# A gated attention and expert block on one core: last steps written out, last roots on VectorE, 77 tiles for 80, first steps reordered

## The reference

```python
# attention, 16 heads of 64, each sequence over its own 64 context rows
q, k, v = layer_norm(layernorm(x)) @ Wq, layer_norm(ctx) @ Wk, layer_norm(ctx) @ Wv
x = x + tanh(g_xattn) * (softmax(q @ k.T / 8) @ v) @ Wo
# one expert of 14 for each token
h = layernorm(x)
e = argmax(h @ router_w); w = softmax(h @ router_w)[e]
x = x + tanh(g_ffn) * w * (gelu(h @ w1[e] + b1[e]) @ w2[e] + b2[e])
```

## Time and profile before

| what | value |
|---|---|
| median of 3 runs | 816.81 us (815.28 to 817.33) |
| the profiled execution | 818.13 us |
| its span, from the first to the last instruction | 816.4 us |
| busy share: PE, PEld | 91%, 84% |
| busy share: DVE, ACT, POOL | 72%, 70%, 60% |
| mean granted TensorE clock | 0.951 of full speed |
| written to and read from memory | 44 MB, 54 GB/s in the mean |

### The profile page before, as it was taken

One profiled execution on the slowest core, in us unless ns is written; L12 is line 12 of the kernel. 1 busy time (PEld: TensorE's weight loads), 2 busy tenths in 40 slices (PEclk: granted clock), 3 DMA queues, 4 the chain that ended last, 5 costly groups with the idle time before them and its releaser, 6 DMA issues. The chain is left out here.

```text
span 816.4 us, 34986 instructions
## 1 busy us (share of the span) xinstructions
PE 746.2 (91%) x12705; PEld 689.3 (84%) x12706; DVE 584.5 (72%) x1580; ACT 571.3 (70%) x1180; POOL 488.4 (60%) x1071
## 2 busy tenths in 40 slices
PE   6779999999999999999999999999999864688884
PEld 6569999999999999999999999999999753588884
DVE  5356678787778787777778787877777853477774
ACT  4557878777778787777787878778877541366663
POOL 2534566666666666666666666666666553277777
PEclk9889999999999999999999999999999965699997
DMA  4840011111101110010010111111000000464540
GB/s 125 235 138 19 20 34 34 31 31 31 31 31 31 31 31 31 31 31 31 31 37 31 37 31 33 36 34 32 25 22 22 23 15 26 127 172 142 143 140 18
DMA packets 50525, 43.90 MB, mean 54 GB/s; under 512 B 14632, under 2 KB 46026, under 8 KB 50474
## 3 DMA queue, kind: packets, MB, share of 16 engines
q1 hardware_dynamic: 43898, 30.53, 13.6%
q0 software_dynamic: 5632, 12.67, 4.4%
q10 hardware_dynamic: 944, 0.01, 0.1%
HBM read 28.55 MB, written 15.68 MB: 54 GB/s over the span
## 5 line engine op out<-in xcount | busy, mean ns | idle before, releaser
L450 POOL TENSOR_TENSOR probs<-probs,row_inv 128x1024 f32<-128x1024 f32 x64 | 122.0, 1907 | 47.2 <-DVE row_inv L1066 46.5
L570 ACT ACTIVATE KT<-psJ 128x512 f32<-128x512 f32 x128 | 76.2, 595 | 56.3 <-PE psJ L742 53.4
L1061 DVE TENSOR_REDUCE row_sum<-probs 128x16 f32<-128x1024 f32 x64 | 77.7, 1215 | 39.0 <-ACT probs L616 39.0
L610 ACT ACTIVATE PTs<-psT 128x512 f32<-128x512 f32 x128 | 75.9, 593 | 37.0 <-PE psT L836 37.0
L1074 DVE TENSOR_TENSOR OT_l<-psO,OT_h 128x1024 fp32r<-128x1024 f32 x64 | 78.1, 1221 | 24.8 <-ACT OT_h L603 24.8
L570 ACT ACTIVATE V<-psJ 128x512 f32<-128x512 f32 x128 | 73.1, 598 | 26.1 <-PE psJ L742 22.8
L616 ACT ACTIVATE probs<-probs 128x1024 f32<-128x1024 f32 x64 | 67.8, 1060 | 24.3 <-DVE probs L1053 24.2
L1046 DVE TENSOR_REDUCE row_max<-psS 128x16 f32<-128x1024 f32 x64 | 75.6, 1181 | 10.1 <-PE psS L799 10.1
L836 PE MATMUL psT<-ident,probs 128*128 128x128 f32 x512 | 79.3, 277 | 3.2 <-POOL probs L450 2.4
L740 PE MATMUL psJ<-CT_h,Wk_h 96*128 96x256 f32 x256 | 78.4, 306 | 2.7 <-ACT QT L570 2.1
L740 PE MATMUL psJ<-XT_h,Wq_h 128*128 128x256 f32 x256 | 77.8, 304 | 3.2 <-ACT QT L570 3.1
(11 more groups left out here) (202 smaller groups left out, 2193.8 us busy)
## 6 DMA issues: line engine op xcount, KB each, us to landing
V<-rows_by_expert SPq DMA_DIRECT2D x40, 129.0 KB
QT<-rows_by_expert SPq DMA_DIRECT2D x40, 129.0 KB, 2.1
x_in<-in_x_dram SPq DMA_DIRECT2D x32, 128.0 KB, 2.1
x_res<-in_x_dram SPq DMA_DIRECT2D x32, 128.0 KB, 2.1
c_in<-in_ctx_dram SPq DMA_DIRECT2D x32, 96.0 KB, 2.3
rows_by_expert<-pad_row SPq DMA_DIRECT2D x1, 1806.0 KB, 11.7
w_sb<-in_L_ffn_w_dram SPq DMA_DIRECT2D x1, 1792.0 KB, 9.6
rows_by_expert<-rows,place_i POOLq DMA_INDIRECT x64, 2.6
```

The source lines that it names most:

```text
L450: pool.tensor_tensor(pr, pr, row_inv[:, p.k % 2, :].unsqueeze(2).to_broadcast([P, 16, SEQ]), ALU.mult).then_inc(s_norm, 1)
L570: act.activation(dst, psJ[n % 2][:, :], ACT.Copy).then_inc(s_jobev, 1)
L610: act.activation(PTs[:, (p.k - 1) % 2, half, :], psT[:, :], ACT.Copy).then_inc(s_ptev, 1)
L1061: dve.tensor_reduce(row_sum[:, :], pr, AX.X, ALU.add).then_inc(s_sum, 1)
```

## The change

It has four parts.

1. **First steps.** In step 0 ScalarE copies jobs 0 and 1 before `norm_in`, and VectorE does `scores_max` and `scores_sub` before `stats_in` and `means_in`. The split of the output weights moves from the end of step 0 to the end of step 2, with raw weights in a buffer of their own, and TensorE's wait for it from the start of step 1 to just before `out_proj` of step 3.
2. **Last steps.** Steps 62 and 63 get an order of their own on TensorE, step 63 on ScalarE too, and steps 64 to 69 are written out piece by piece on all engines (`D64` to `D69`). `router` and `rank` of group 29 and `post_b`, `router` and `rank` of group 30 work in the bank `psJ[1]`, which the jobs no longer need.
3. **Last roots.** The roots of groups 30 and 31 are taken by VectorE (`last_roots`: 12 instructions on two columns) and no longer by GpSimd.
4. **77 tiles.** `TILES` is the most that 8192 tokens in 14 experts can fill, 77, and no longer rounded up to 80: one trip written out, three in the loop, and 13 tiles with the drain written out.

The function `spin` (products on the identity, to keep TensorE at work) is only moved; it is called ahead of the front part, as before, and nowhere behind it.

```diff
-    TILES = -(-(TOK // P + E - 1) // RING) * RING
+    TILES = (TOK + E * (P - 1)) // P
+    TRIPS = TILES // RING
...
-        raw_v, raw_o = Vf[0:C, HALF:HALF + INNER], Vf[:, HALF + INNER:HALF + 2 * INNER]
+        raw_v, raw_o = Vf[0:C, HALF:HALF + INNER], sb("raw_o", [P, M8 * D])[:, :]
...
-            for u in range(LOOP_TO, STEPS_U):
+            for u in range(LOOP_TO, GROUPS // 2):
...
+        D64, D65, D66, D67, D68, D69 = (Plan(GROUPS // 2 + n // 4, n % 4) for n in range(6))
...
-            with eng.Fori(1, TILES // RING) as v:
+            with eng.Fori(1, TRIPS) as v:
...
-            words = entries(engine, expert_tab, TILES // PACK - 1, 1, 2 ** 16 - 1)
-            for i in range(4):
-                ffn(TILES + i, TILES // RING, i, [i - n < 0 for n in range(5)], experts(words, i))
+            words = entries(engine, expert_tab, TRIPS * (RING // PACK) - 1, RING // PACK + 1, 2 ** 16 - 1)
+            for t in range(TRIPS * RING, TILES + 4):
+                ffn(t, t // RING, t % RING, [t - n < TILES for n in range(5)], experts(words, t - TRIPS * RING))
...
@@ GpSimd @@
+            send(D65)
+            send(D67)
+            send(D69)
+            with pool.Fori(0, TRIPS) as v:
                 for i in range(RING):
                     send_out(v * RING + i, i, v)
+            for t in range(TRIPS * RING, TILES):
+                send_out(t, t % RING, TRIPS)
...
@@ ScalarE, norm_x2 @@
+                if p.fixed and p.g >= GROUPS:
+                    bias, scale = shift4[p.g - GROUPS][:, 0:2], rstd4[p.g - GROUPS][:, 0:2]
+                    act.wait_ge(s_rootx, 13 * (p.g - GROUPS + 1))
...
@@ ScalarE, step @@
-                if p.odd:
+                if p.fixed and p.s == PAIRS - 1:
+                    norm_x2(p)
+                    values_high(p)
+                    probs_out(p, 0)
+                    probs_out(p, 1)
+                    norm_T(p)
+                    expo(p)
+                    attn_out(p)
+                elif p.odd:
...
-                    norm_in(p)
+                    if not (p.fixed and p.s == 0):
+                        norm_in(p)
                     values_high(p)
                     job(p, 0)
                     job(p, 1)
+                    if p.fixed and p.s == 0:
+                        norm_in(p)
                     expo(p)
...
-                    if p.fixed and p.s == 0:
+                    if p.fixed and p.s == 2:
                         high(3)
...
@@ ScalarE, behind the front part's steps @@
+            values_high(D64)
+            route_exp(D64)
+            probs_out(D64, 0)
+            probs_out(D64, 1)
+            values_high(D65)
+            norm_x2(D65)
+            attn_out(D65)
+            norm_T(D65, psJ[1])
+            route_exp(D66)
+            norm_x2(D67)
+            norm_T(D67)
+            route_exp(D68)
...
@@ TensorE, step @@
-                    if p.fixed and p.s == 1:
-                        pe.wait_ge(s_wl, 4)
+                if p.fixed and p.s == PAIRS - 1:
+                    scores(p)
+                    value_sums(p)
+                    probs_T(p, 0)
+                    probs_T(p, 1)
+                    post_b(p)
+                    out_proj(p)
+                elif p.fixed and p.s == PAIRS - 2:
+                    scores(p)
+                    value_sums(p)
+                    pe.wait_ge(s_jobev, 12 * GROUPS)
+                    post_a(p)
+                    probs_T(p, 0)
+                    router(p)
+                    probs_T(p, 1)
+                    rank(p)
...
+                    if p.fixed and p.s == 3:
+                        pe.wait_ge(s_wl, 4)
                     out_proj(p)
...
@@ TensorE, behind the front part's steps @@
+            misc[1] = (s_jobev, 12 * GROUPS)
+            value_sums(D64)
+            post_a(D64)
+            router(D64, 1)
+            probs_T(D64, 0)
+            probs_T(D64, 1)
+            rank(D64, 1)
+            value_sums(D65)
+            out_proj(D65)
+            post_b(D65, 1)
+            post_a(D66)
+            router(D66, 1)
+            rank(D66, 1)
             pe.wait_ge(s_bias, 32)
             pe.wait_ge(s_ptev, 2 * PAIRS)
             pe.transpose(psT[:, 0:E * FK], b1_rows[:, :], ident[0:E * FK, 0:E * FK]).then_inc(s_b1T, 1)
+            post_b(D67)
+            router(D68)
+            rank(D68)
+            misc_free()
...
@@ VectorE, step @@
-                    stats_in(p)
-                    means_in(p)
+                    if not (p.fixed and p.s == 0):
+                        stats_in(p)
+                        means_in(p)
                     scores_max(p)
                     scores_sub(p)
+                    if p.fixed and p.s == 0:
+                        stats_in(p)
+                        means_in(p)
...
-                    if p.fixed and p.s == 0:
+                    if p.fixed and p.s == 2:
                         low(3)
...
+            def last_roots(p):
+                i = p.g - GROUPS
+                nw0, nq0, rstd0, shift0, n = nw4[i][:, 0:2], nq4[i][:, 0:2], rstd4[i][:, 0:2], shift4[i][:, 0:2], 13 * i
+                dve.wait_ge(s_agg2, 2 * (p.g - 1))
+                dve.tensor_scalar(nw0, mv[:, 4:6, 1], EPS, None, ALU.add).then_inc(s_rootx, 1)
+                dve.wait_ge(s_rootx, n + 1)
+                dve.tensor_scalar(rstd0.bitcast(I32), nw0.bitcast(I32), -0.5, RSQRT_SEED, ALU.mult, ALU.add).then_inc(s_rootx, 1)
...
@@ VectorE, behind the front part's steps @@
+            values_low(D64)
+            residual(D64)
+            means_x2(D64)
+            route(D64, psJ[1])
+            places(D64, psJ[1])
+            weight(D65)
+            values_low(D65)
+            last_roots(D64)
+            residual(D66)
+            means_x2(D66)
+            last_roots(D66)
+            route(D66, psJ[1])
+            places(D66, psJ[1])
+            weight(D67)
+            route(D68)
+            places(D68)
+            weight(D69)
```

More of the change, by code:

```diff
@@ L363, in load_rows, with load_trip @@
                 sp.dma_start(tile_rows[i], rows_dram[bass.ds(r, P), :]).then_inc(f_load[i], 16)
-            def load_trip(v):
-                for i in range(RING):
+            def load_trip(v, count):
+                for i in range(count):
                     if i % PACK == 0:
@@ L623, in attn_out, with norm_T @@
                 act.activation(aT[:, :], psM[:, 0:GT], ACT.Copy, scale=tanhs[:, 0:1]).then_inc(s_aT, 1)
-            def norm_T(p):
+            def norm_T(p, bank=psM):
                 if p.group(2) is None:
@@ L862, in post_a, with post_b @@
                 misc[0] = (s_x2, p.g - 1)
-            def post_b(p):
+            def post_b(p, b=0):
                 if p.group(2) is None:
                     return
-                misc_free()
+                misc_free(b)
                 pe.wait_ge(s_n2, 2 * (p.g - 1))
                 for t in range(2):
-                    last = pe.transpose(psM[:, P * t:P * t + P], rows[:, p.par(), t, D:2 * D], ident[:, :])
+                    last = pe.transpose(banks[b][:, P * t:P * t + P], rows[:, p.par(), t, D:2 * D], ident[:, :])
@@ L898, in step, with spin @@
+            def spin(n, bank):
+                for _ in range(n):
+                    pe.matmul(bank[:, 0:P], ident[:, :], ident[:, :], start=True, stop=True)
             def step(p):
@@ L935, in step @@
                     job(p, 7)
-            def spin(n):
-                for _ in range(n):
-                    pe.matmul(psO[:, 0:P], ident[:, :], ident[:, :], start=True, stop=True)
             pe.wait_ge(s_cc, 2)
-            spin(13)
+            spin(13, psO)
             prep(Plan(-1, 0))
-            spin(10)
+            spin(10, psO)
             for n in range(10):
@@ L1138, in weight, with places @@
                 dve.tensor_scalar(rows[:, par, :, 2 * D], inv[:, :], tanhs[:, 1:2], None, ALU.mult).then_inc(s_route, 1)
-            def places(p):
+            def places(p, bank=psM):
                 if p.group(3) is None:
```

80 lines of the change are left out of this document (48 added, 32 removed).

## The result

| | median | runs | ratio to before, 95% interval |
|---|---|---|---|
| before | 816.04 us (814.69 to 817.33) | 4 | |
| after | 806.91 us (806.71 to 807.31) | 4 | 0.9889 (0.9870 to 0.9908) |

The change takes 9.1 us off; 806.1 was predicted.

What follows compares the result with a forecast made beforehand. TensorE was taken to set the pace from 56 to 640 us, GpSimd's scatters the end. -6.5 - 0.3 - 3.9 = -10.7 us from the profiled 818.13 gives 807.4, as median 806.1 us; range 804 to 808.5, chance 0.60.

Steps and rivals of the forecast that it cites:

- The start, -6.5 forecast: Steps 0 to 3: earlier job 4, no stand for `Wo_l` and less half clock take 6.5 us off.
- the lower of the two sums, 5.7: Start: 1.7 (job 4) + 3.0 (`Wo_l` stand) + 1.0 (clock), if the first half-clock stretch still ends at 43.3.
- The upper sum, 7.2: Start: up to 1.5 us more than 5.7, if the first half-clock stretch ends earlier.
- the warning that a gain beyond 7 us would run into the load of group 4: Step 2: its next load, `x_in` and `c_in`, is behind the pad rows and would limit a start gain beyond 7 us.
- part of the start only: Rival: lower clock case (5.7), and a load or `Wo_l` costs 2 us; start 3.7, total 808.9 us; chance 0.18.
- Wo's wait and its new place: Step 1's stand of 2.98 us goes; the wait in step 3 costs nothing, or 2 us without VectorE's cover.
- Last steps, -0.3 forecast: Steps 63 to 69: order +1.5, roots on VectorE -2.4, `route_exp` before the norm +0.6; bounds -3 and +2.
- last steps better: Rival: reordered last steps keep TensorE at full clock, -3 instead of -0.3, total 803.4 us; chance 0.13.
- 77 tiles, -3.9 forecast: Expert part: GpSimd's scatters set the end, so three fewer at 1.286 us each take 3.9 us off.
- TensorE's gap before the straight tiles: Expert part: gap before the last 13 tiles stays as at other trips; either way the sum stays -3.9.
- The rival of 827 us: Slower: without idle products TensorE stays at half clock through the experts' first two trips (32 tiles); chance of slower 0.03.
- The signs: New-profile checks, including step 2 scores at 46 to 48 us and the loop's end about 6.5 us earlier.

Runs made afterwards that it cites:

- start_spin: Changed kernel plus nine idle products in TensorE's stand of step 0, behind job 3: median 807.80 us, ratio to before 0.9882.
- best: Changed kernel plus act_order's ScalarE order, tail_spin's idle products and start_spin's nine: median 802.81 us, ratio to before 0.9820.
- both_spin: The kernel best plus six idle products in TensorE's stand ahead of job 4 of step 2: median 802.09 us, ratio to before 0.9803.
- act_order: Changed kernel with ScalarE's last probabilities copies and last norm put ahead of the router exponentials: median 806.43 us, ratio to before 0.9853.
- tiles_77: Kernel before with only the 77 tiles in place of 80: median 812.87 us, ratio to before 0.9959.
- half_scatter: Changed kernel without the scatters of the odd tiles, whose output rows stay unwritten: median 799.50 us, ratio to before 0.9769.
- wo_later: Kernel before with only the split of Wo and TensorE's wait for it moved two steps later: median 812.74 us, ratio to before 0.9956.
- last_steps: Changed kernel with the start and tiles of before, so only the last steps and last roots change: median 814.77 us, ratio to before 0.9984.
- act_tail: Changed kernel plus both act_order's ScalarE order and tail_spin's idle products: median 802.65 us, ratio to before 0.9816.
- roots_pool: Changed kernel with the last two square-root columns back on GpSimd in place of VectorE: median 808.73 us, ratio to before 0.9892.
- tail_spin: Changed kernel plus idle products in TensorE's waits of the last steps and the expert table: median 806.27 us, ratio to before 0.9857.

## Why the prediction was right, point by point

*The start, -6.5 forecast.* Against the trace of before it is -5.5 (37.00 to 31.49). Term by term, in the trace: job 4 was to come 1.7 us sooner and comes 1.86 (8.50 us behind scores 0 instead of 10.36); the stand of 2.98 went whole; at scores 1 the gain is 5.70 (13.03 instead of 18.73), so the half clock gave 0.86. That is the lower of the two sums, 5.7, and of it 0.2 are lost by scores 3. The mis-sized term in the trace is the clock's: the choice of the upper end, "since the work after job 4 is now unbroken", was wrong, for with unbroken work from 37.54 on the clock fell at about 39 and came back at 46. The upper sum, 7.2, came true in three other traces with this start, which had 3.4 us at half clock instead of 6.8 and took 29.8 us. And the warning that a gain beyond 7 us would run into the load of group 4 held in start_spin, best and both_spin. But all these sums start from the trace of before, whose 37.00 us and 10.2 us at half clock are long for this code: the two halves alone gave -0.65 and -3.6 us by the ratios, -1.2 and -4.1 by the medians. Over many executions the start is worth 4.3 to 5.3 us, not 6.5, and by the ratios it is as near to the rival "part of the start only" (-3.7) as to the forecast.

*Wo's wait and its new place.* Right: the stand is gone, the split at 61.38 delays VectorE's maximum of step 3, and the loop is as long as before.

*Last steps, -0.3 forecast.* Measured -1.3 by the stretches, within the bounds of -3 and +2. The order is the mis-sized term, the roots were right. Against the front's shift of 4.5 us (scores of step 62 at 642.86 and 638.34), `out_proj` of group 30 came 1.9 us late as forecast, but `out_proj` of group 31 only 0.65 (673.21 to 669.34) and not 1.5. Of the difference, 0.6 us lie in `out_proj` of group 30: begun later, it met the full clock after 2.8 us of its work, where it was at half for 4.4 us before, and took 4.3 us instead of 4.9. This is the rival "last steps better" in small. The roots took 2.4 us (677.07 to 679.47) as forecast, and GpSimd's in their place put 1.7 us on the path to the norm. `route_exp` ahead of the norm cost 0.5 (forecast 0.6). That it also stands ahead of the probabilities' copies was seen and priced as part of the +1.5; the price was a stand of 3.46 us, of which act_order gets some 1.1 us back.

*77 tiles, -3.9 forecast.* Right: -3.93 where it is alone. In the changed kernel the stretch is 5.15 shorter; the other 1.2 are gaps between early scatters (0.85 and 1.36 before, one of 0.68 after), which vary from trace to trace with the same code. Two readings behind the term were off. From 727.67 to 813.80 there are 66 steps, not 67, so the mean is 1.305 us, and two of them are late by 0.4 and 0.25; back to back it is 1.29, which leaves the -3.9 as it is. And TensorE's gap between trips isn't free in the first of them, as tiles_77 shows. GpSimd's lag behind VectorE's last tile didn't shrink by 0.9 us but grew from 6.3 to 6.8. No run shows the up to 1.5 us allowed for the start of its straight code; the choice of 0 was right: the scatters run at 1.29 us to the end, and half_scatter shows that they do set the end.

*TensorE's gap before the straight tiles.* Forecast to stay, as the rows of before had it, and it stays: 2.57 us at 776.65 beside 2.39 to 3.02 at the three others. The Trainium skill's rule (Runtime: NRT & Kernel Launch, Instruction fetch mechanics), by which code that is run straight is fetched ahead and a taken branch out of the fetched pages is what stalls, would by itself have taken it away; here the measurement decides, and no run shows whether the register loads that precede the tiles make it.

*No idle products ahead of the experts.* The rival of 827 us was far off: the clock is back at 701.3, 5.9 us behind the first tile's start. But idle products had a use that the prediction did not look for: in other waits they bring 1.9 us.

*The signs.* No stand for `Wo_l`, later `value_sums` and `out_proj` against the loop's end (27.8 and 31.0 us behind the scores of step 62 instead of 26.7 and 30.4), 12 small VectorE instructions in 2.4 us and 77 scatters at 1.29 us without a gap after the first trip: all as said. The distance from the loop to the first tile changed by 1.3 us, under the 3 that would have refuted it. Two signs missed: the scores of step 2 came at 49.16, not at 46 to 48, and the loop's end 4.5 us earlier, not 6.5. Of these 2.0 us, 1.15 lie ahead of the scores of step 0, which came later in this trace, and 1.0 is the start's shortfall (0.16 came back in the loop).

*The total.* The three terms make -10.7 of a profiled execution, and the spans differ by 10.8; the medians differ by 9.1 (7.5 to 10.6). The prediction took the whole -10.7, read off one of before's longer executions, from the median: 1.6 us too much. A fourth execution of before brought its median from 816.81 down to 816.04, and so the error left is 0.8 us. That the total fits better than its terms is luck, in the traces as well: along them the differences are +1.15 ahead of the scores of step 0, -5.5 in the start, -0.2 in the loop, -1.35 in the last steps, -5.15 between the scatters and +0.2 behind them. The start was put 1 us too high, the last steps 1 us and the scatters 1.2 us too low, and the later scores of step 0, which nobody forecast, took the rest back.

What stays open: what, beside a stand, decides whether and for how long the clock falls. In wo_later, last_steps and tiles_77 it didn't fall behind a stand of 3.04 to 3.06 us in step 0, where it did in before (3.08). And the same code with the same stand has 6.8 us at half clock in some executions (after, act_order, act_tail) and 3.4 in others (roots_pool, tail_spin, half_scatter). The time of scores 0 doesn't tell them apart, 27.90 us in act_order and 27.86 in tail_spin. And act_tail's median is 4.3 us under the changed kernel's, where the last steps account for 3.3 in the mean of three traces; the rest is within the intervals.

## What to carry to other kernels

Before a stand is filled or removed, look for what comes next that doesn't move with it: here a load, whose landing the new order doesn't bring forward, let some 7 us of gain through and no more, and behind the wait that it made the clock fell at a later place. Cut the traces into stretches with landmarks that all kernels share, since a stretch of 30 us with the same code differs by 1.7 to 2.2 us between executions with the clock, and look whether the profiled execution is a fast or a slow one of its kernel. An engine sets the end only once it has fallen behind the others: look at the first trips of a loop by themselves. And when steps are written out by hand, let no engine's short instruction that waits for a long chain stand ahead of a copy that TensorE needs: one exponential of 0.23 us cost a stand of 3.46 us, and some 1.1 us of the kernel's time.

## What the runs showed of the hardware

- Filling a stand of 2.4 us with idle products kept the granted clock at 1.00 there, and it fell to 0.50 some 20 us later, 1.2 us behind the end of a stand of 2.38 us (start_spin) and at the end of one of 2.33 us (best). Where that stand was filled too it stayed at 1.00 (both_spin, one trace).
- The stretches at half clock in the start were 3.4, 6.8 or 10.2 us long, with the same code 3.4 in one trace and 6.8 in the next.
- With TensorE unbroken at work the clock was at half from about 39 to 46 us in the changed kernel; it was at 1.00 in the stand (36 to 38) and fell behind it.
- Behind a stand of 3.04 us in the same step the clock stayed at 1.00 in wo_later (36 to 44).
- Behind TensorE's gap of 2.46 us between the first two trips of experts the clock was at 0.50 for 3.4 us in before; behind one of 2.40 us it stayed at 1.00 in wo_later, and the scatters took 2.35 us less.
- The load of `c_in` of group 4, issued behind the pad rows, landed 7.1 to 8.8 us after its issue in the 14 traces; the median of all loads of `c_in` is 2.2 to 2.4 us.
- An indirect scatter of 128 rows holds GpSimd for 0.98 us and the next follows 0.30 us later, at 1.29 us each, whether they are in a loop or in straight code.
- The 20 idle products at the very start took 3.33 us in the trace of before and 4.48 in that of after, which shifts all that follows: the landmark *scores 0* varies by 2 us over the 14 traces, whose work ahead of it is the same.
